# A pre-norm decoder layer on one core: another calling sequence on all five engines, fewer filler products, finer waits, a bf16 bound

## What is computed

```python
x = x + attn(layernorm(x))      # 16 heads of 32; k, v through rank 8, rotary, 8-bit grid over all of k and of v
                                # windows of 128, step 64: sigmoid scores, divided by their sum, blended
x = x + wkv(w, u, layernorm(x), ctx)   # scan over 256 tokens: decayed sums p, q; y = (A p + E v) / (A q + E)
h = silu(bit_linear(ln(x), w_gate)) * bit_linear(ln(x), w_up)
x = x + bit_linear(rms_norm(h, ln_weight), w_down)

def weight_quant(w):
    s = 1.0 / clip(mean(abs(w)), EPS, None)
    return clip(round(w * s), -1.0, 1.0) / s
```

## Time and profile before

| | us |
|---|---|
| median of 3 executions | 1010.95 (1007.66 to 1012.41) |
| the profiled execution | 1009.94 |
| its span, first to last instruction | 1008.4 |
| TensorE clock granted, mean | 0.981 of full |

### The profile page before, as it was taken

The page is one execution under the profiler, slowest core; times in us unless marked ns, Lnnn a source line. Parts: engine busy times, 40 slices in busy tenths (PEclk is TensorE's granted clock), DMA queues, the critical chain, the costliest instruction groups (busy, mean ns, idle before and its releaser), DMA issues.

```text
span 1008.4 us, 22772 instructions
## 1 busy us (share of the span) xinstructions
PE 915.4 (91%) x8736; PEld 560.8 (56%) x8736; DVE 859.0 (85%) x1551; ACT 665.2 (66%) x1161; POOL 456.5 (45%) x510
## 2 busy tenths in 40 slices
PE   6997989889898989998999898999989998987898
PEld 3456667665564646565555555555555555553454
DVE  4767866788889899898989898989898989898874
ACT  1257362495958686777777777768686859595653
POOL 1202203145363646464646364645545464636452
PEclk9999999989999999999999999999999999999999
DMA  9978360111223332424242322323232232322223
GB/s 365 411 262 335 100 210 2 45 49 32 71 85 81 96 82 90 87 84 91 85 90 87 82 95 65 106 55 89 71 82 90 66 105 72 95 64 73 53 63 84
DMA packets 119388, 107.21 MB, mean 106 GB/s; under 512 B 91792, under 2 KB 94720, under 8 KB 118128
## 3 DMA queue, kind: packets, MB, share of 16 engines
q1 hardware_dynamic: 116320, 100.64, 33.2%
q10 hardware_dynamic: 2336, 2.52, 0.8%
q0 software_dynamic: 624, 2.59, 0.7%
HBM read 65.62 MB, written 10.75 MB: 76 GB/s over the span
## 4 chain that ended last, share of the span: by engine, by line
PE 32%; ACT 20%; POOL 14%; DVE 13%; issue 12%; DMA 2%; SPq 1%; DVEq 0%; POOLq 0%; ACTq 0%
PE bank L557 11%; POOL sums L1832 6%; PE bank L665 6%; PE bank L645 5%; ACT arena L946 5%; PE bank L576 4%; POOL work L1849 4%; PE bank L657 3%; ACT L950 2%; ACT junk L1001 2%; DVE amax L1472 2%; ACT sums L967 2%; POOL sums L1880 2%; DVE junk L1494 1%; DMA work<-work 1%
## 5 line engine op out<-in xcount | busy, mean ns | idle before, releaser
L1849 POOL TENSOR_TENSOR work<-junk,lnw 128x512 f32<-128x512 f32 x128 | 181.9, 1440 | 168.4 <-DVE junk L1494 146.9
L645 PE MATMUL bank<-w_up_gate,qT 128*128 128x512 bf16 x1024 | 240.4, 381 | 14.4 <-DVE junk L1494 7.1
L645 PEld LDWEIGHTS bank<-w_up_gate,qT 128*128 128x128 bf16 x1024 | 95.5, 98 | 129.0 <-DVE junk L1494 13.7
L985 ACT ACTIVATE work<-work,fs 128x2048 f32<-128x2048 f32 x32 | 64.1, 2004 | 112.4 <-DVE fs L1516 112.4
L665 PE MATMUL bank<-w_down,work 128*128 128x512 bf16 x512 | 124.8, 390 | 10.9 <-ACT junk L1001 7.9
L946 ACT ACTIVATE arena<-bank 128x384 f32<-128x384 f32 x256 | 104.9, 496 | 36.7 <-PE bank L576 36.4
L1006 ACT ACTIVATE junk<-junk,deq 128x512 f32<-128x512 f32 x128 | 92.3, 722 | 42.6 <-DVE junk L1494 42.6
L607 PE MATMUL bank<-wo_sb,wide 128*128 128x512 f32 x256 | 114.4, 600 | 2.4 <-DVE wide L1397 2.4
L557 PE MATMUL bank<-wide,wq_sb 128*128 128x256 f32 x512 | 114.3, 381 | 2.4 <-DVE rows L1404 1.8
L1494 DVE TENSOR_TENSOR junk<-bank,junk 128x512 f32<-128x512 f32 x128 | 86.1, 683 | 31.8 <-ACT junk L1001 21.4
L557 PEld LDWEIGHTS bank<-wide,wq_sb 128*128 128x128 f32 x512 | 96.1, 190 | 25.4 <-issue 12.8
(11 more groups left out here) (154 smaller groups left out, 1594.8 us busy)
## 6 DMA issues: line engine op xcount, KB each, us to landing
sums<-in_xT SPq DMA_DIRECT2D x8, 1024.0 KB, 10.7
wide<-in_xT SPq DMA_DIRECT2D x16, 512.0 KB, 3.8
wide<-wide SPq DMA_DIRECT2D x64, 128.0 KB, 2.1
out<-rows SPq DMA_DIRECT2D x32, 256.0 KB, 2.5
rows<-in_x SPq DMA_DIRECT2D x15, 512.0 KB, 3.7
ctx_T<-in_ctxT SPq DMA_DIRECT2D x15, 512.0 KB, 4.5
kv_b<-k_raw SPq DMA_DIRECT2D x64, 96.0 KB, 2.3
work<-in_wgT SPq DMA_DIRECT2D x4, 1024.0 KB, 19.0
```

The source lines that it names most:

```text
L645: last = te.matmul(bank[4 + k % 4][:, :], qT[:, c, t * P:(t + 1) * P], w_up_gate[:, m, c, cols], start=c == 0, stop=c == NC - 1)
L1849: ge.tensor_tensor(hid_w[:, t, cols], hid[:, n % 2, :], lnw[:, cols], op=ALU.mult).then_inc(z_set.sem, 1)
```

## The change

The functions change in four places, and all five lists of calls are new. The functions first:

```diff
@@ sync_program, turn_hidden
             sy.wait_ge(h_quant.sem, h_quant.at(f, t))
-            if f:
+            if f == 0:
+                sy.wait_ge(w_tern[DOWN].sem, w_tern[DOWN].at(0))
+            else:
                 sy.wait_ge(down_made.sem, down_made.at(f - 1, t))
@@ vector_program, round_weights
-            ve.tensor_scalar(w_chunk(m, k), w_chunk(m, k), MAGIC + 1.0, MAGIC - 1.0, ALU.min, ALU.max).then_inc(
-                w_bound[m].sem, 1)
-            ve.wait_ge(w_bound[m].sem, w_bound[m].at(0, k))
             if m == DOWN and k == 0:
                 for trig in trig_stored:
                     ve.wait_ge(trig.sem, trig.at(1))
-            ve.tensor_scalar(tern_dst[m][:, k, :], w_chunk(m, k), MAGIC, None, ALU.subtract).then_inc(
+            ve.tensor_scalar(tern_dst[m][:, k, :], w_chunk(m, k), MAGIC + 1.0, MAGIC, ALU.min, ALU.subtract).then_inc(
+                w_bound[m].sem, 1)
+            ve.wait_ge(w_bound[m].sem, w_bound[m].at(0, k))
+            ve.tensor_scalar(tern_dst[m][:, k, :], tern_dst[m][:, k, :], -1.0, None, ALU.max).then_inc(
                 w_tern[m].sem, 1)
@@ vector_program, hidden_round
             if f:
                 for k in both:
                     ve.wait_ge(hid_turned[t][k].sem, hid_turned[t][k].at(f - 1))
+            else:
+                ve.wait_ge(w_tern[DOWN].sem, w_tern[DOWN].at(0, 2))
@@ pool_program, weigh_hidden
-            elif t == 0 and n == 0:
-                ge.wait_ge(w_tern[DOWN].sem, w_tern[DOWN].at(0))
+            elif n == 0:
+                ge.wait_ge(w_tern[DOWN].sem, w_tern[DOWN].at(0, t))
                 ge.wait_ge(large_loads.sem, large_loads.at(0))
@@ tensor_program, two of the many lines of the list
         queries(1, 1)
         wkv_keys(0)
-        spin(0, 0, 12)
+        spin(0, 0, 16)
```

492 lines of the change are left out of this document (245 added, 247 removed).

## The result

The kernel after takes 1001.77 us (median of 4 executions, 1000.62 to 1002.28), the kernel before 1010.21 beside it (4 executions, 1007.66 to 1012.41). The ratio is 0.9913, with a 95% interval from 0.9892 to 0.9935: 0.9% faster. The forecast was 995.5 with a range from 983 to 1009. Direction and range held, the gain is 8.4 us where 15.4 were forecast, and the parts came out quite otherwise.

A forecast was written before the change was run, and what follows sets the result against it. It took PE and DVE as both nearly full in the loop, with slack and filler in the fill. 0 - 2 - 6 - 6 - 5.4 + 1 + 3 = -15.4 from 1009.9 gave 994.5, plus 1.0 to the median 995.5; range 983 to 1009.

The forecast's parts named there:

- The first 67 us: Start up to the queries of sequence 0: PE's work unchanged by the new load order; 0, from -2 to +3.
- Queries 0 to 1: Fill: five products ahead of queries(1, 0) gone, then the residual of sequence 0 on DVE is late; -2, from -4 to 0.
- The bf16 bound: Weight rounding on DVE: third instruction, now bf16 to bf16, takes 0.7 us instead of 1.23; counted only inside the stages.
- Queries 1 to 2: Fill, 66.5 us: filler products fall from 79 to 39, down-matrix sum earlier, queries(2, 0) less delayed; -6, from -12 to 0.
- this piece is not shortened: Queries 1 to 2: POOL's stretch from the addition over partitions to the blend only moves 2.7 us earlier.
- Queries 2 to 3: Fill, 61.2 us: ACT loses 7 of 13 table loads, DVE is late next; -6, from -13 to -2.
- The loop: 12 turns: keys_grid takes 0.35 us every time, other moves 0; -0.45 a turn, -5.4 in all.
- The same collision again, not two: Loop: refine at the start of POOL's outputs meets one collision of 0.9 us, as either kind of turn had before.
- the first rival: Loop gives more: refine always first, its collision with outputs goes too, 1.2 us a turn, 986 us; chance 0.15.
- The drain: After the loop: moves cancel or win -1.5, last two down halves without filler cost 2.5; +1, from -2 to +4.
- The clock: Fill: with fewer filler products, more pieces run at half the granted clock; +3, from 0 to +10.
- the one on the fill: Rival: POOL's piece, DVE's transfer waits or cold pieces take half of the 14 us; 1008, no change; chance 0.10.

The follow-up runs named there:

- the second experiment: Kernel after with load_keys(0) on SyncE put back behind the last column load, the query load and three GATE loads; 998.41 us, ratio 0.9902.
- the third experiment: Kernel after with 40 products that nobody reads added back between queries 1 and queries 2; 1006.13 us, ratio 0.9962.

## The prediction against the result, step by step

- **The first 67 us, 0** (to +3): +1.6, and +3.4 at the end of the first queries. The step looked at PE's work and at the columns' load, and took the moved `load_keys(0)` for one DMA call among others. Its own wait, and the six loads behind it, are the cost; the second experiment gets 3 us back.
- **Queries 0 to 1, -2:** +1.4 (47.94 for 46.55); -0.4 if one counts from the end of `queries(0, 0)`, which took 1.8 longer for want of its input. The term for the five products held: in the kernel before `attention_out(0, 1)` and the first half of `residual(0)` were both over at 111.65, and the queries started 2.0 us later, behind the products. What failed is that the residual would come no later. It came 4.8 us later (115.77 for 110.95): 5.3 from GpSimd's sum, less the 0.5 of the cheaper rounding. As the step says, the residual then set queries 1; what sets the residual is that sum, 5.8 us behind GpSimd's last ordinary instruction. That pause stood in the trace of before and in none of my rows.
- **The bf16 bound, third instruction 0.7 us:** 0.69.

```profile
L1303 DVE TENSOR_SCALAR w_up_gate<-w_up_gate x8: 693/694/696, 86.0 to 143.2; 128x2048 bf16<-128x2048 bf16 x8
```

  The Trainium skill, VectorE: DVE Perf Modes, has 693 ns for a bf16 copy of this size, in the section on the TRN2 errata; the trace agrees, with a median of 694. The price was right, and alone it is worth nothing measurable.
- **Queries 1 to 2, -6:** 0. The term "the last sum 2.7 us earlier" failed: it came 4.5 later, 1.5 of it within the stage. I stepped through PE and ACT, and ACT's sum was held by its load, which was held by a rounding on DVE behind a `rotate` that waits for a swap. The term "this piece is not shortened" failed too; it got 1.9 longer. The term of 3 us for fillers ahead of `queries(2, 0)` held: from the end of `attention_out(1, 1)` it is 2.4 us now and was 5.9; the third experiment gives it back with the opposite sign. `attention_out(1, 0)` at 4.44 for 3.60 is what the clock took there, and `wkv_back(0, 0)` and `wkv_back(0, 1)` took 0.85 longer for the same reason. In sum within the stage: +1.5 for the sum, +1.9 for the pause, +0.7 for what stands behind it, -2.2 for the 13 products ahead of `wkv_back` (166.30 for a blend that ended at 164.38), +1.7 for the clock and -3.5 for those ahead of the queries, which is +0.2. (The working also misread the filler's pieces: the first of its seven, 5.34 us, starts at 121.43 and not at 129.83.)
- **Queries 2 to 3, -6:** -1.6. The table loads fell from 13 to 6 as forecast:

```profile
L1001 ACT ACT_TABLE_LOAD x3 | 3.8, 1283 | 7.9 <-PE bank L647 7.9
L992 ACT ACT_TABLE_LOAD x1 | 1.3, 1283 | 0.8 <-PE bank L619 0.8
L946 ACT ACT_TABLE_LOAD x1 | 1.3, 1283 | 0.8 <-PE bank L578 0.8
L950 ACT ACT_TABLE_LOAD x1 | 1.3, 1283 | 0.0
```

  But ACT was not what bound. DVE was, as the step itself warned ("that leaves some 55"): I took its busy time of before and forgot that instructions get longer where the moved ones meet GpSimd. GpSimd runs from 187.96 to 194.28 without a gap now, and two instructions of the rounding `DOWN, 1` that start at 191.06 and 193.04 take 1.95 and 2.33 us for 1.28 and 1.23. A cold piece cost part of the rest:

```profile
231.65 1.07 PE L628 MATMUL bank<-ident,sums 128*128 128x128 f32 x8 [2.42 <-DVE sums L1395]
232.55 3.55 PE L647 MATMUL bank<-w_up_gate,qT 128*128 128x512 bf16 x8
```

  8 products at half clock, 3.55 us for 1.89, right ahead of `attention_out(2, 0)`. In the run with the drain's fillers back, which has the same fill, the clock stayed up here, and the stage took 58.25 us for 59.6.
- **The loop, -5.4:** -8.1. `keys_grid` at its bare length in every turn held. "The same collision again, not two" was mis-sized: DVE's collision went, one of GpSimd's came, as in the first rival but with 0.34 a turn from this piece, not 1.2. And 0 for all other moves was wrong by 0.39 a turn. Three products instead of one cost nothing in idle time, as the step says, but kept the clock up, which it had not priced as a gain.
- **The drain, +1:** -0.8 (133.0 from queries 15 to the last output, for 133.8). The last 16 products took 3.61 us as before; the cold ones were those of t = 0. The step priced cold products at the very end and did not ask which of them wait for a transfer anyway.
- **The clock, +3:** in the fill it is 0.87 from queries 1 to 2 and 0.97 from queries 2 to 3. The second is better than before, and the loop won by it. The cold pieces on the chain named above come to 3.4 us, near the 3; but they lie inside the stages, and the loop's gain isn't in the term. Queries 3 after 236 was the sign named for being wrong, and it came: the steps for the fill are wrong. The turn under 52.3 came too. So it is in part luck that the total lies in the range (it is just outside the 990 to 1001 that had the chance of 0.50). No rival describes what happened: the one on the fill takes half of its 14 us, and a further 6 whose source the working doesn't give, and the one on the loop takes the fill as forecast. Errors met: the fill gave +0.4 instead of -14, and against these 14.4 us stand 2.7 more from the loop, 1.8 more from the drain, and the 3 that I had added for the clock beside the stages, whose lengths hold it already.
